# A two-layer mixture-of-experts kernel on one core: the routing gate of the first four tiles made in two halves, and the high parts of one routed step made by VectorE

## The reference

```python
# layer 0 (B=32, L=128, D=128, rank 16)
z = ((x @ v) / 128) @ u.T / 16
x = x + gelu(x @ W.T + fc_bias + z + cond)              # erf gelu
# layer 1 (E=4, H=512), head/wrist/proprio = three parts of the 128 tokens
gate_in = concat(full_mean, head_proprio_mean, wrist_proprio_mean)
logits = (gate_in @ gate_w + gate_b) * (1 + scale) + shift
scores = softmax(logits);  w_be = the two largest, normalised, else 0
for e in range(4):                                      # expert 1 without wrist, expert 2 without head tokens
    out += w_be[:, e] * mask[e] * (gelu_tanh(x @ ew1[e] + eb1[e]) @ ew2[e] + eb2[e])
out += gelu_tanh(x @ sw1 + sb1) @ sw2 + sb2
return x + out
```

## Time and profile before

| what | value |
|---|---|
| median of 3 runs | 241.7 us (241.41 to 241.79) |
| the profiled execution | 240.64 us, span in the trace 238.4 us |
| TensorE busy | 230.7 us, 97% of the span |
| VectorE busy | 200.5 us, 84% |
| ScalarE busy | 142.6 us, 60% |
| GpSimd busy | 19.4 us, 8% |
| granted TensorE clock | 1.000 over the span |

### The profile page before, as it was taken

The page is one execution under the profiler, slowest core; times in us unless marked ns, Lnnn a source line. Parts: engine busy times, 40 slices in busy tenths (PEclk is TensorE's granted clock), DMA queues, the critical chain, the costliest instruction groups (busy, mean ns, idle before and its releaser), DMA issues.

```text
span 238.4 us, 3425 instructions
## 1 busy us (share of the span) xinstructions
PE 230.7 (97%) x1194; PEld 197.0 (83%) x1194; DVE 200.5 (84%) x456; ACT 142.6 (60%) x279; POOL 19.4 (8%) x46
## 2 busy tenths in 40 slices
PE   8999988999999999999999999999999999999995
PEld 8887676788788887888888887888888889899894
DVE  0489999999896867976899999995999989778883
ACT  3699998817965097744977079443654075553531
POOL 8000000024000010002000030002000030020000
PEclk9999999999999999999999999999999999999999
DMA  6895000000010000100010000100010000100011
GB/s 174 235 313 135 1 1 0 3 0 0 3 44 0 0 0 4 44 0 1 3 43 1 3 0 1 44 0 3 0 44 0 3 0 1 44 3 1 0 44 44
DMA packets 11256, 7.40 MB, mean 31 GB/s; under 512 B 3776, under 2 KB 10600, under 8 KB 11240
## 3 DMA queue, kind: packets, MB, share of 16 engines
q1 hardware_dynamic: 10760, 7.07, 10.1%
q10 hardware_dynamic: 288, 0.10, 0.2%
q0 software_dynamic: 192, 0.03, 0.1%
HBM read 5.09 MB, written 2.10 MB: 30 GB/s over the span
## 4 chain that ended last, share of the span: by engine, by line
PE 76%; DVE 11%; ACT 10%; issue 2%; POOL 0%; DVEq 0%; ACTq 0%; POOLq 0%
PE ps L522 23%; PE ps L524 22%; PE ps L523 22%; ACT h L428 4%; DVE hs_lo L816 2%; PE ps L528 2%; ACT L428 2%; ACT L409 2%; PE ps L540 2%; PE ps L571 1%; ACT W_raw L414 1%; PE ps L665 1%; DVE segsum L791 1%; PE ps L579 1%; DVE hs_lo L834 1%
## 5 line engine op out<-in xcount | busy, mean ns | idle before, releaser
L428 ACT ACTIVATE h<-ps,b_col 128x512 f32<-128x512 f32 (+1 forms) x160 | 90.5, 639 | 58.8 <-PE ps L524 55.7
L834 DVE SCALAR_TENSOR_TENSOR hs_lo<-h,w_be,hs_hi 128x344 fp32r<-128x344 f32 (+1 forms) x124 | 73.6, 656 | 0.0
L522 PE MATMUL ps<-x_hi,W_hi 128*128 128x512 f32 (+2 forms) x168 | 65.8, 392 | 1.8 <-ACT h L428 0.6
L524 PE MATMUL ps<-x_lo,W_hi 128*128 128x512 f32 (+2 forms) x168 | 60.7, 362 | 0.0
L523 PE MATMUL ps<-x_hi,W_lo 128*128 128x512 f32 (+2 forms) x168 | 60.7, 361 | 0.0
L522 PE MATMUL ps<-hs_hi,W_hi 128*128 128x512 f32 (+1 forms) x156 | 57.3, 367 | 1.1 <-DVE hs_lo L816 0.7
L524 PE MATMUL ps<-hs_lo,W_hi 128*128 128x512 f32 (+1 forms) x156 | 56.9, 365 | 0.0
L523 PE MATMUL ps<-hs_hi,W_lo 128*128 128x512 f32 (+1 forms) x156 | 56.6, 363 | 0.0
L826 DVE TENSOR_SCALAR hs_hi<-h,w_be 128x344 fp32r<-128x344 f32 (+1 forms) x120 | 45.0, 439 | 8.3 <-PE ps L524 4.1
L522 PEld LDWEIGHTS ps<-x_hi,W_hi 128*128 128x128 f32 x168 | 31.7, 189 | 10.6 <-ACT h L428 2.9
L523 PEld LDWEIGHTS ps<-x_hi,W_lo 128*128 128x128 f32 x168 | 31.7, 189 | 4.4 <-issue 1.0
(11 more groups left out here) (121 smaller groups left out, 177.2 us busy)
## 6 DMA issues: line engine op xcount, KB each, us to landing
W_raw<-in_L_cond_ew SPq DMA_DIRECT2D x8, 256.0 KB, 6.4
out<-x_tok SPq DMA_DIRECT2D x7, 256.0 KB, 2.2
x_tok<-in_x SPq DMA_DIRECT2D x3, 512.0 KB, 5.8
x_tok<-in_x SPq DMA_DIRECT2D x2, 256.0 KB, 3.4
W_raw<-in_L_cond_sw SPq DMA_DIRECT2D x2, 256.0 KB, 4.8
out<-x_tok SPq DMA_DIRECT2D x2, 128.0 KB, 1.7
F_pad<-in_fside_Bx1x1024x SPq DMA_DIRECT2D x2, 64.0 KB, 6.1
W_raw<-in_L_cond_W ACTq DMA_DIRECT2D x1, 64.0 KB, 2.9
```

Of the source, the lines that this page charges most:

```text
L428: ins = nc.scalar.activation(span(h[:, k % 3, c, :], s), up_bank(k, c), ACT.Gelu_apprx_tanh, bias=b1_col[:, s, c:c + 1])
L522: nc.tensor.matmul(dst, w_hi, m_hi, start=start, stop=False)
L524: return nc.tensor.matmul(dst, w_hi, m_lo, start=False, stop=stop)
L834: nc.vector.scalar_tensor_tensor(lo[:, :, c], h[:, k % 3, :, c], w_be[:, t * NB + b, s - 1:s], f32(hi[:, :, c]), ALU.mult, ALU.subtract).t ...
```

## The change

`GATES` now starts with (0, 2), (2, 4). The first gate's chain moves forward on VectorE, in front of split(0) and split(1); the new second gate takes part in the main loop by `late_gate`. The high part of step 2 is made by VectorE.

```diff
-    GATES = [(0, 4), (4, 6), (6, 8)]
+    GATES = [(0, 2), (2, 4), (4, 6), (6, 8)]
-    ACT_HI = (2,)
+    ACT_HI = ()
@@ ScalarE
             gelu(0)
+            gate_tanh(0)
             gelu(1)
-            gate_tanh(0)
@@ TensorE
             up(0)
-            up(1, range(CH // 2))
+            up(1, range(1))
             logits(0)
-            up(1, range(CH // 2, CH))
+            up(1, range(1, CH))
@@ VectorE, gate_in
-                dve.wait_ge(segsum_ok, NSEG * (g + 3))
+                dve.wait_ge(segsum_ok, NSEG * (g + 2))
@@ VectorE, the order
                 if t == 2:
                     x1_low(0)
                     segment_sums(1, 2)
+                    gate_in(0)
                     weight_low(WEIGHTS[3])
-                residual(t)
-                if t == 2:
-                    output_rows()
+                if t < NA - 1:
+                    residual(t)
+            output_rows()
             x1_low(1)
-            segment_sums(2, 4)
-            gate_in(0)
             dve.wait_ge(bias_in, 16 * 3)
             modulation()
-            split(0)
+            residual(NA - 1)
             read_logits(0)
             gate_maximum(0)
             gate_ranks(0)
+            split(0)
+            gate_weights(0)
             split(1)
-            gate_weights(0)
             weight_low(WEIGHTS[4])
             weight_low(WEIGHTS[5])
@@ VectorE, main loop, in step k = 3
                 g = late_gate(k, 1)
                 if g is not None:
+                    if GATES[g][1] == NA:
+                        segment_sums(*GATES[g])
                     gate_in(g)
```

## The result

The changed kernel takes 240.32 us (median of 4, 239.86 to 240.53) against 241.57 us for the kernel before (median of 4). The ratio is 0.9944, 95% interval 0.9929 to 0.9959: 1.0 to 1.7 us less. Measured again on another chip with seven executions it was 0.995 (0.9933 to 0.9968).

What follows compares the result with a forecast made beforehand. TensorE works nearly all the span, and its early waits mostly hang on VectorE's length of work. Through VectorE's ledger the gain at down(6) is 1.16 us, kept to the end: 241.7 - 1.2 = 240.5 us, range 239.9 to 241.3.

Steps and rivals of the forecast that it cites:

- VectorE as the clock of 22 to 58 us: VectorE has no idle bracket from 22 to 57.28 us; the change is worth what it does to VectorE's length there.
- ledger: VectorE's distances between starts, one entry per edit: split(0) +1.03, split(1) -0.24, end of split(2) -1.12, end of split(5) +0.5 us.
- The new wait: TensorE at down(5): a wait of 0.7 us for VectorE, which releases at 57.91, replacing the old waits.
- down(2): Step 2's down matmuls on TensorE: released by VectorE at 39.98 us, 1.12 us earlier, with a wait of 0.6 us left.
- xT(4): Tile 4's transposes on TensorE: start at 42.81 instead of 44.24 us, -1.43, as ScalarE's copies end near 41.3.
- down(6): Step 6's down matmuls on TensorE: start at 62.8 us, -1.16, a gain kept to the end.
- No wait between 64 us and the tail: TensorE from 64 us on: the changed profile would show no wait before the tail.
- The slower rival: VectorE sets the end, since ScalarE's 1.6 us of work goes to an engine without idle time: +0.49, 242.2 us; chance 0.06.

Runs made afterwards that it cites:

- hi4_on_act: The changed kernel with step 4's high part made on ScalarE: 239.63 us, ratio 0.9947 to the kernel before.
- gates_again: The changed kernel with step 2's high part back on ScalarE, leaving only the gate's edits, second run: 239.5 us, ratio 0.9923 to the kernel before.
- hi_only: The kernel before with one edit, step 2's high part on VectorE: 242.12 us, ratio 1.0082.
- sums_at_8: The changed kernel with the sums of tiles 2 and 3 repeated on VectorE at step 8 into a new, unread tile: 241.3 us, ratio 1.0001 to before.
- tile_64: The changed kernel with one unused tile of 64 bytes a partition before gate_terms: 240.94 us, ratio 0.9987 to the kernel before.

## Why the prediction was right

**VectorE as the clock of 22 to 58 us: right, and shown.** Each ledger entry was met within 0.05 us, since their prices came from instructions of the same shape in a full stream. The doubled sums move the end by nearly their whole length at step 3 and by nearly nothing at step 8, so the waits at down(4) and down(5) are the places where VectorE's length turns into time.

**The new wait: right.** The forecast had a wait of 0.5 to 0.8 us at down(5); it is 0.59, and hi4_on_act, which takes it away, gains 0.4 by its trace. At down(2) the wait is 0.40, where the forecast had 0.6; the start is where it was forecast.

**xT(4): right.** Its old wait hung on ScalarE's copies; they now end at 40.94 + 1.13 = 42.07 in the trace, and xT(4) starts at 43.65 straight behind down(2). gates_again shows that L443's departure wasn't needed for this: with L443 kept, the copies hold xT(4) by 0.25 us, and it still starts at 20.56 from the zero against 20.75.

```profile
24.96 1.28 ACT L428 ACTIVATE h<-ps,b_col 128x512 f32<-128x512 f32 x2
26.10 0.26 ACT L452 ACTIVATE tanh_g<-logit_x 128x32 f32<-128x32 f32 x1
...
38.94 1.94 ACT L428 ACTIVATE h<-ps,b_col 128x344 f32<-128x344 f32 x4 [0.89 <-PE ps L524]
...
40.94 1.13 ACT L396 ACTIVATE W_raw<-ps 32x128 f32<-32x128 f32 x4
```

The tanh (ScalarE of the changed kernel, above) starts 3.20 us from the zero, where 25.24 - 22.04 had put it, with no idle before it.

**down(6): the term was slightly off, and luck made up for it.** Forecast -1.16, measured -1.04; up(8) took 63.78 - 61.77 = 2.01 us against the 1.92 of the sum, because its first matmul, behind the new logits matmul, takes 0.25 us to the next start instead of 0.16. The rest came to -0.96; the last tenth goes in small pieces that I did not follow. The medians in turn fell by 1.25 us. That 240.32 came so near to the forecast's 240.5 is in part luck: the sum was 0.2 us too large, and the early microseconds of the prologue favoured the changed kernel's executions by about 0.3. The forecast met this chance in the 1.1 us by which the profiled execution lay under the median, and carried it over as a constant. The -0.96 lies at the edge of the ratio's interval (1.0 to 1.7 us) and inside that of the repeat (0.8 to 1.6 us).

**"No wait between 64 us and the tail": misread.** Both kernels have the two waits of 0.21 us for ScalarE's GELU near 90 and 145 us; the forecast's reading of the kernel before had left them out too. They cost the gain nothing: counted from the zero, these matmuls start 1.00 and 0.97 us earlier than before.

**What the prediction didn't ask: which half of the change earns it.** It took the whole change through one ledger, where the high part stood as +1.58. The slower rival was right in its first sentence: work went from an engine with room to one without. It was outweighed by the gate. By the ledger, halving it put 1.37 us of sums off from the prologue to step 3 and took 0.82 + 0.42 us of small instructions out of VectorE's way. Alone on the old kernel the high part makes it slower (hi_only); undone in the changed kernel it makes that faster. Of the gate's edits only the tanh's place was run apart; what the halving, the deferred sums and the new order bring each is argued from the ledger. **The gate's edits alone are the best kernel of this study**, 0.7 us under the changed one on the same chip; with step 4's high part on ScalarE too, the rest is the same within 0.02 us.

## What to carry to other kernels

Where one engine has no idle time over a stretch and the busiest engine waits for it there, write a ledger of starts for that engine with one entry per edit and read it off at each point of meeting; take the prices from full streams of the same shape. Then price each half of a change by itself, since a good half can carry a bad one. And compare traces from a common instruction behind the prologue, not by their spans; an experiment must not move tiles, so write scratch results into a tile that is there.

## What was not expected of the hardware

- **96 unused bytes changed the pace of the matmuls that read the tiles behind them.** 234, 233, 234 instead of 231, 228, 231 ns from start to start, 1.1 us over the kernel. 64 bytes: 233, 232, 233 ns, 0.7 us of the rest. The rule is open.
- **A wait of 2.00 us was followed by a fall of TensorE's clock** to 0.50 for some three microseconds, in the one traced execution; two of the other six have the same mean clock and time, and four don't. Behind waits up to 0.8 us the traces show none. That the wait is the cause is not shown: one of twelve executions of sums_at_8 (242.72 us) and one of 17 of the kernel before, beside tile_64 (242.82 us), had a granted clock of 0.991 too, without a trace, and the kernel before has no such wait in its own.
- **GpSimd and VectorE hold each other up, and which one loses turns on who starts first.** Before, GpSimd began tile 1's biases at 57.36, ahead of VectorE's casts (L809) at 57.66: GpSimd took 2.23 us for its three instructions, and the casts 1.60.

```profile
57.36 2.23 POOL L363 TENSOR_TENSOR x<-x,bias 128x168 f32<-128x168 f32 x3 [3.40 <-DVE hs_lo L834]
...
57.66 1.60 DVE L809 CAST hs_hi<-h 128x1024 fp32r<-128x1024 f32 x2 [0.38 <-ACT h L428]
```

  After, the casts start at 58.54 and GpSimd's first of three instructions at 58.70; that one alone took 4.33 us, while the casts kept their 1.28:

```profile
58.54 1.28 DVE L809 CAST hs_hi<-h 128x1024 fp32r<-128x1024 f32 x2
59.74 2.35 DVE L816 TENSOR_TENSOR hs_lo<-h,hs_hi 128x1024 fp32r<-128x1024 f32 x2
...
58.70 4.33 POOL L363 TENSOR_TENSOR x<-x,bias 128x168 f32<-128x168 f32 x1 [3.41 <-DVE hs_lo L834]
```

  TensorE waited for none of it. The Trainium skill, on the page SBUF — State Buffer, section Who interferes with whom, says that whoever of the two starts first keeps the shared ports for its whole instruction and the other is fully blocked. The trace agrees as to who loses, with 0.30 us between the two starts before and 0.16 us after. It also shows a hold over more than one instruction: the casts end at 59.82 and the subtractions (L816) behind them at 62.09, and GpSimd's instruction only at 63.03.
